# New instruction lists for the prologue and the first FFN half of a fused mixer and FFN kernel

## The reference

```python
uv = layernorm(x) @ in_proj_w + in_proj_b        # 512 -> 1024
u, v = uv[..., :512], uv[..., 512:]
v = silu(v); v_local = depthwise_conv3(v) + conv_b
h_t = a * h_(t-1) + ssm_b * v_local_t            # a = sigmoid(logit_a), along the rows
y = ssm_c * h + ssm_d * v_local
out = (u * silu(y)) @ out_proj_w + out_proj_b
attn = layernorm(out + layernorm(x)) * ln_w + ln_b
x = x + layernorm(attn)
z = gelu(layernorm(x) @ ternary(W1).T + b1)      # 512 -> 2048
x = x + layernorm(z @ ternary(W2).T + b2)        # 2048 -> 512
```

## Time and profile before

| what | value |
|---|---|
| time, median of 3 runs | 1447.07 us (1446.5 to 1452.28) |
| the profiled execution: its time | 1446.71 us |
| its span | 1444.7 us |
| busy PE, DVE, ACT, POOL | 97%, 77%, 61%, 30% |
| TensorE's mean granted clock | 0.995 of full speed |
| chain that ended last, by engine | PE 83%, DVE 6%, issue 4%, ACT 3% |

### The profile page before, as it was taken

The page is one execution under the profiler, slowest core; times in us unless marked ns, Lnnn a source line. Parts: engine busy times, 40 slices in busy tenths (PEclk is TensorE's granted clock), DMA queues, the critical chain, the costliest instruction groups (busy, mean ns, idle before and its releaser), DMA issues.

```text
span 1444.7 us, 18964 instructions
## 1 busy us (share of the span) xinstructions
PE 1402.6 (97%) x6492; PEld 637.3 (44%) x6492; DVE 1118.3 (77%) x1891; ACT 875.7 (61%) x1261; POOL 432.2 (30%) x522
## 2 busy tenths in 40 slices
...
GB/s 253 216 56 66 52 88 30 34 84 30 59 30 74 44 30 74 19 84 30 39 79 30 59 30 88 30 30 81 19 77 30 44 74 30 29 1 30 59 30 30
DMA packets 155984, 82.00 MB, mean 57 GB/s; under 512 B 132720, under 2 KB 132720, under 8 KB 155760
## 3 DMA queue, kind: packets, MB, share of 16 engines
...
## 4 chain that ended last, share of the span: by engine, by line
PE 83%; DVE 6%; issue 4%; ACT 3%; DMA 1%; POOL 1%; SPq 1%; DVEq 0%; POOLq 0%; ACTq 0%
PE f1b L534 14%; PE f1b L535 14%; PE f2b L562 13%; PE f2b L563 13%; PE misc L501 6%; PE misc L503 6%; PE misc L502 6%; PE misc L514 3%; PE misc L515 3%; PE misc L516 3%; DVE bn L696 1%; DVE tp L820 1%; POOL rsc L1624 1%; ACT ring L1293 1%; SPq L405 1%
## 5 line engine op out<-in xcount | busy, mean ns | idle before, releaser
L562 PE MATMUL f2b<-w,ring 128*128 128x512 fp8e5 x1008 | 382.7, 380 | 5.5 <-DVE w L1004 4.9
L563 PE MATMUL f2b<-w,ring 128*128 128x512 fp8e5 x1008 | 382.7, 380 | 0.0
L534 PE MATMUL f1b<-x3T,w 128*128 128x512 f16 x960 | 364.8, 380 | 4.0 <-DMA x3T<-tp 1.3
L535 PE MATMUL f1b<-x3T,w 128*128 128x512 f16 x960 | 364.8, 380 | 0.0
L1283 ACT ACTIVATE ring<-f1b,par 128x512 f32<-128x512 f32 x256 | 175.1, 684 | 249.7 <-PE f1b L535 249.4
L1623 POOL TENSOR_SCALAR ve<-mv 128x4 f32<-128x4 f32 (+2 forms) x89 | 33.7, 379 | 728.2 <-DVE mv L706 727.8
L714 DVE SCALAR_TENSOR_TENSOR ring<-ring,f_sc 128x512 f16<-128x512 f32 x256 | 208.8, 830 | 41.6 <-ACT ring L1293 41.6
L1293 ACT ACTIVATE ring<-ring,f_sc 128x512 f16<-128x512 f32 x256 | 180.4, 711 | 0.0
L501 PE MATMUL misc<-x1T,win_hi 128*128 128x512 f16 x464 | 175.9, 379 | 2.4 <-DVE yb L807 1.4
L502 PE MATMUL misc<-x1T,win_hi 128*128 128x512 f16 x464 | 175.9, 379 | 0.0
L503 PE MATMUL misc<-x1T,win_lo 128*128 128x512 f16 x464 | 175.9, 379 | 0.0
...
## 6 DMA issues: line engine op xcount, KB each, us to landing
...
x1T<-tp SPq DMA_TRANSPOSE x68, 3.1
...
```

The lines of the kernel that those rows point to most:

```text
L534: pe.matmul(b[:, :], w, src[:, k, :], start=k == 0, stop=False)
L535: mm = pe.matmul(b[:, :], w, src[:, KC + k, :], start=False, stop=k == KC - 1)
L562: pe.matmul(f2b[q][:, :], h_hi[:, i % H_SLOTS, qs], w2[:, j, :], start=j == 0, stop=False)
L563: mm = pe.matmul(f2b[q][:, :], h_lo[:, i % H_SLOTS, qs], w2[:, j, :], start=False, stop=j == FC - 1)
```

## The change

All five lists up to the second tile's u groups are written out instruction by instruction in a new order. On SP both u halves of `in_proj_w` are issued after all four transposes of tile 0, and the transposes of tile 1 ahead of `out_proj_w`, tile 2 and the first piece of W1; `load_w2(3)` goes behind the transposes of tile 2. On PE `warm` is called for 42 instead of 24 matmuls, the sum for the u half follows the second v group of tile 0, and the first FFN half has an order of its own (`first_ffn`). On DVE the chains are cut into named steps (`step` and `after` replace `link`), placed between other work; `wo_scale` no longer computes `o_inv`, which `wo_back` does later. Step 2's first half on DVE and ACT is listed instead of being sorted. Chunk 0 alone of W2 goes ahead of chunks 8 to 11 of W1. POOL computes the statistics of tile 0's blocks 2 and 3 together, and those of tile 2 after the edges. The core of the diff:

```diff
-ORDER = ([(W1_CHUNK, i) for i in range(8)] + [(W2_CHUNK, i) for i in range(4)] + [(W1_CHUNK, i) for i in range(8, 12)]
-         + [(W2_CHUNK, i) for i in range(4, 12)] + [(W1_CHUNK, i) for i in range(12, 16)]
-         + [(W2_CHUNK, i) for i in range(12, 16)])
-SIGNED = (1, 1, 1, 1, 2, 2, 2, 2, 3, 4, 5, 6, 7, 7, 7, 7, 8, 8, 8, 8, 9, 9, 9, 9, 10, 10, 10, 10, 11, 11, 11, 11)
-FIRST, SECOND = range(8, 21), range(28, 32)
-AT_TERNARY = {8: 1.19, 9: 2.25, 10: 3.3, 11: 3.5, 12: 5.11, 13: 5.12, 14: 5.7, 15: 5.75, 16: 6.3, 17: 6.4, 18: 6.6, 19: 7.4, 20: 7.6,
-              28: 11.55, 29: 11.6, 30: 11.65, 31: 14.55}
-AT_SIGN_C, AT_SIGN_Q, AT_SIGN_G, AT_SIGN_LAST = (0.5, 1.5, 2.5, 3.5), 4.4, (5.3, 6.5), 10.15
+ORDER = ([(W1_CHUNK, i) for i in range(0, 8)] + [(W2_CHUNK, i) for i in range(0, 1)]
+         + [(W1_CHUNK, i) for i in range(8, 12)] + [(W2_CHUNK, i) for i in range(1, 12)]
+         + [(W1_CHUNK, i) for i in range(12, 16)] + [(W2_CHUNK, i) for i in range(12, 16)])
+SIGNED = (1, 1, 1, 1, 2, 2, 2, 2, 3, 4, 4, 4, 4, 5, 6, 7, 8, 8, 8, 8, 9, 9, 9, 9, 10, 10, 10, 10, 11, 11, 11, 11)
+SECOND = range(28, 32)
+AT_TERNARY = {28: 11.55, 29: 11.6, 30: 11.65, 31: 14.55}
+AT_SIGN_LAST = 10.15
...
-for j in range(NB):
-    transpose("t1", 0, j)
-    if j < 2:
-        sp.dma_start(wf[:, 2 * j:2 * j + 2, 0:D], w_in_d[:, 2 * j:2 * j + 2, 0:D]).then_inc(winu_in[j], 16)
+transposes("t1", 0)
+for i in range(2):
+    sp.dma_start(wf[:, 2 * i:2 * i + 2, 0:D], w_in_d[:, 2 * i:2 * i + 2, 0:D]).then_inc(winu_in[i], 16)
+transposes("t1", 1)
 sp.dma_start(wo_raw, w_out_d).then_inc(wout_in, 16)
 load_x(2)
-transpose("t1", 1, 0)
 load_w1(0)
-for j in range(1, NB):
-    transpose("t1", 1, j)
 load_w1(1)
+sp.dma_start(row[:, :, :], rows.partition_broadcast(P)).then_inc(row_in, 16)
 load_w1(2)
-sp.dma_start(row[:, :, :], rows.partition_broadcast(P)).then_inc(row_in, 16)
 load_w1(3)
...
 load_w2(2)
-load_w2(3)
 transposes("t1", 2)
 load_w2(0)
 load_w2(1)
+load_w2(3)
 load_x(3)
...
     if (kind, t, b) == ("v", 1, 0):
         pe.wait_ge(par_ok, 4)
+    if (kind, t, b) == ("v", 1, 1):
         pe.wait_ge(scale_ok, 3)
...
-def setup_in_proj():
-    pe.wait_ge(x1_hi, 1)
-    warm(6)
-    pe.wait_ge(pmx, KC + 1)
-    pe.matmul(win_sum_bank(1), ones[:, :], wm_sq[:, 1, :], start=True, stop=True).then_inc(pm1, 1)
-    warm(6)
+def win_sum(half_):
+    pe.wait_ge(pmx, (KC + 4, KC + 1)[half_])
+    pe.matmul(win_sum_bank(half_), ones[:, :], wm_sq[:, half_, :], start=True, stop=True).then_inc(pm1, 1)
+def keep_warm():
     pe.wait_ge(x1_lo, 3)
-    warm(12)
-    pe.wait_ge(pmx, KC + 4)
-    pe.matmul(win_sum_bank(0), ones[:, :], wm_sq[:, 0, :], start=True, stop=True).then_inc(pm1, 1)
+    warm(14)
+    for k in (1, 3):
+        pe.wait_ge(win_l, k)
+        warm(8)
...
+def first_ffn():
+    f1(0, 0)
+    f1(0, 1)
+    f1(0, 2)
+    f1(0, 3)
+    f1(0, 4)
+    f1(0, 5)
+    f1(0, 6)
+    f2(0, 0)
+    f1(0, 7)
+    f1(0, 8)
+    f2(0, 1)
+    f2(0, 2)
+    f2(0, 3)
+    f2(0, 4)
+    f2(0, 5)
+    f2(0, 6)
+    f2(0, 7)
+    in_proj("u", 1, 2, u_mm)
+    in_proj("u", 1, 3, u_mm)
+    f2(0, 8)
...
 ffn_scale()
-setup_in_proj()
-for b in range(KC):
-    in_proj("v", 0, b, v_mm)
-for b in range(KC):
-    in_proj("v", 1, b, v_mm)
-    if b == 0:
-        wo_sum()
-for b in range(KC):
-    in_proj("u", 0, b, u_mm)
-for j in range(NB):
-    if j == NB - 1:
-        threshold(0)
-    o(0, j)
-for b in range(KC):
-    in_proj("v", 2, b, v_mm)
+pe.wait_ge(x1_hi, 1)
+warm(6)
+win_sum(1)
+warm(6)
+keep_warm()
+in_proj("v", 0, 0, v_mm)
+in_proj("v", 0, 1, v_mm)
+win_sum(0)
+in_proj("v", 0, 2, v_mm)
+in_proj("v", 0, 3, v_mm)
+in_proj("v", 1, 0, v_mm)
+in_proj("v", 1, 1, v_mm)
+in_proj("v", 1, 2, v_mm)
+wo_sum()
+in_proj("v", 1, 3, v_mm)
...
+o(0, 3)
+threshold(0)
...
+    steps[name] = len(steps) + 1
+def after(name):
+    ve_.wait_ge(prep, steps[name])
...
+        ve_.wait_ge(wo_sc_ok, 2)
...
 setup_params()
-for j in range(NB):
-    x_stats(0, j)
-    aggr(0, 0, j)
+x_stats(0, 0)
+aggr(0, 0, 0)
+x_stats(0, 1)
+x_stats(0, 2)
+aggr(0, 0, 1)
+x_stats(0, 3)
+aggr(0, 0, 2)
 win_max_v(0)
+aggr(0, 0, 3)
 win_max_v(1)
+win_max_v(2)
+win_max_v(3)
 t_lo("t1", 0, 0)
-win_max_v(2)
+win_square(1)
 t_lo("t1", 0, 1)
-win_max_v(3)
-win_square(1)
-t_lo("t1", 0, 2)
-win_scale(1)
-t_lo("t1", 0, 3)
+win_total(1)
 x_stats(1, 0)
-setup_split(0)
+win_power(1)
 x_stats(1, 1)
+win_bound(1)
 aggr(0, 1, 0)
 aggr(0, 1, 1)
-setup_split(1)
+win_scale(1)
+t_lo("t1", 0, 2)
 x_stats(1, 2)
-setup_split(2)
+t_lo("t1", 0, 3)
 x_stats(1, 3)
 aggr(0, 1, 2)
+setup_split(0)
 aggr(0, 1, 3)
+setup_split(1)
+setup_split(2)
+setup_split(3)
+t_lo("t1", 1, 0)
 v_scale()
-setup_split(3)
+t_lo("t1", 1, 1)
 win_max_u(0)
+t_lo("t1", 1, 2)
 win_max_u(1)
+t_lo("t1", 1, 3)
 win_square(0)
-t_lo("t1", 1, 0)
+taps(0, 0, True)
+win_total(0)
+win_power(0)
+win_bound(0)
 win_scale(0)
-t_lo("t1", 1, 1)
-t_lo("t1", 1, 2)
-setup_split(KC)
+ffn_total()
+taps(0, 1, True)
+setup_split(KC + 0)
+setup_split(KC + 1)
+ffn_exponent()
+ffn_inverse()
 ffn_scale()
-t_lo("t1", 1, 3)
+setup_split(KC + 2)
+taps(0, 2, True)
+gate_exponent()
 u_bias()
+gate_inverse()
+gate_shift()
+setup_split(KC + 3)
+gate_scale()
+gate_largest()
+taps(0, 3, True)
 x_stats(2, 0)
-setup_split(KC + 1)
-for j in range(1, NB):
-    x_stats(2, j)
-for j in range(NB):
-    aggr(0, 2, j)
-setup_split(KC + 2)
-gate_scale()
-taps(0, 0, True)
-taps(0, 1, True)
-setup_split(KC + 3)
-taps(0, 2, True)
-wo_scale()
+x_stats(2, 1)
...
+wo_norm()
+aggr(0, 2, 2)
+aggr(0, 2, 3)
 scan(0, 0)
 taps(0, 1, False)
+wo_total()
 y(0, 0)
-setup_out_proj(1)
+wo_power()
+taps(0, 2, False)
+wo_bound()
 scan(0, 1)
-taps(0, 2, False)
+wo_inverse()
+scan(0, 2)
 y(0, 1)
 taps(0, 3, False)
-setup_out_proj(2)
-scan(0, 2)
-ve_.wait_ge(par_ok, 8)
+wo_scale()
+ve_.wait_ge(par_ok, 5)
 gate(0, 0)
 y(0, 2)
-gate(0, 1)
+setup_out_proj(0)
...
+ternary(2)
+ternary(3)
+taps(1, 0, True)
+ternary(4)
+taps(1, 0, False)
+taps(1, 1, True)
+ternary(5)
+threshold_mean(1)
+scan(1, 0)
 threshold(1)
+y(1, 0)
 ternary(6)
 ternary(7)
+taps(1, 1, False)
+ternary(8)
+taps(1, 2, True)
+lo(0, 0)
+scan(1, 1)
+lo(0, 1)
+y(1, 1)
+taps(1, 2, False)
+ternary(9)
+ternary(10)
+ternary(11)
+ternary(12)
+ternary(13)
+ternary(14)
+scan(1, 2)
+lo(0, 2)
+y(1, 2)
+lo(0, 3)
+ternary(15)
+ternary(16)
+lo(0, 4)
+ternary(17)
+lo(0, 5)
+taps(1, 3, True)
+lo(0, 6)
+ternary(18)
+lo(0, 7)
+taps(1, 3, False)
+ternary(19)
+lo(0, 8)
+ternary(20)
+scan(1, 3)
+y(1, 3)
+gate(1, 0)
+gate(1, 1)
...
-        act.wait_ge(abs_ok, 6)
+        act.wait_ge(abs_ok, 8)
...
+t_hi("t1", 1, 3)
+silu_v(0, 0)
+centre_tap(0, 0)
+silu_v(0, 1)
+centre_tap(0, 1)
+split_in(KC + 0)
 split_in(KC + 1)
-silu_v(0, 0)
+silu_v(0, 2)
+split_in(KC + 2)
+centre_tap(0, 2)
+split_in(KC + 3)
+silu_v(0, 3)
+centre_tap(0, 3)
+silu_v(1, 0)
...
-t_hi("t1", 2, 2)
-front(2, 3)
+centre_tap(1, 0)
 abs_sum(4, 6, w2_raw[2], w2_in[2])
-centre_tap(1, 0)
-abs_sum(5, 7, w2_raw[3], w2_in[3])
+centre_tap(1, 1)
 sign_w1(0)
+abs_sum(5, 4, w2_raw[0], w2_in[0])
+abs_sum(6, 5, w2_raw[1], w2_in[1])
+silu_v(2, 0)
+abs_sum(7, 7, w2_raw[3], w2_in[3])
+silu_v(2, 1)
 sign_w1(1)
-centre_tap(1, 1)
-silu_v(2, 0)
-abs_sum(6, 4, w2_raw[0], w2_in[0])
-silu_v(2, 1)
 silu_v(2, 2)
-abs_sum(7, 5, w2_raw[1], w2_in[1])
-centre_tap(1, 2)
 silu_v(2, 3)
...
+copy_x3(7)
+load_table(1, ACT.Gelu)
+d_conv(1, 0)
+gelu(0, 0)
+centre_tap(1, 2)
+hi(0, 0)
+gelu(0, 1)
+sign_first(0)
+gelu(0, 2)
+hi(0, 1)
+hi(0, 2)
+gelu(0, 3)
+d_conv(1, 1)
+gelu(0, 4)
+sign_w1(2)
+gelu(0, 5)
+hi(0, 3)
+sign_first(1)
+sign_first(2)
+gelu(0, 6)
+d_conv(1, 2)
+sign_first(3)
+hi(0, 4)
+sign_w2(1)
+centre_tap(1, 3)
+gelu(0, 7)
+hi(0, 5)
+hi(0, 6)
+hi(0, 7)
+gelu(0, 8)
+hi(0, 8)
+sign_w2(2)
+d_conv(1, 3)
+silu_y(1, 0)
...
+rstd_first(0)
+rstd_first(1)
+rstd_x(0, slice(2, NB), front_rs)
 rstd_x(1, slice(0, 2), front_rs)
 rstd_x(1, slice(2, NB), front_rs)
 weight_bound()
 gate_bound()
+first_edge(0)
+first_edge(1)
+first_edge(2)
+first_edge(3)
+first_left()
 rstd_x(2)
-for b in range(KC):
-    first_edge(b)
-pool.tensor_copy(v[:, 1, :, 0:1], v[:, 0, :, TT:TT + 1]).then_inc(left_ok, 1)
-for b in range(KC):
-    keep_state(0, b)
-halves = slice(0, 2), slice(2, NB)
-for i, js in enumerate(halves):
-    rstd(1, 0, rsc[:, 0, js], True, js, (half_ok[1], rs_ok[1])[i])
-for i, js in enumerate(halves):
-    rstd_b_half(js, (half_ok[2], rs_ok[2])[i])
-for i, js in enumerate(halves):
-    rstd(3, 0, rsc[:, 2, js], True, js, (half_ok[3], rs_ok[3])[i])
+keep_state(0, 0)
+keep_state(0, 1)
+keep_state(0, 2)
+keep_state(0, 3)
+rstd_a_half(0)
+rstd_a_half(1)
+rstd_b_half(0)
+rstd_b_half(1)
+rstd_c_half(0)
```

More of the change, by code:

```diff
@@ L635, in _ @@
             pe.wait_ge(h_ok, NB)
-            for n in range(len(halves_x3)):
-                transpose_x3(n)
-                if n == 3:
-                    threshold(1)
+            transpose_x3(0)
+            transpose_x3(1)
+            transpose_x3(2)
+            transpose_x3(3)
+            transpose_x3(4)
+            threshold(1)
```

(31 more changed lines are left out.)

327 lines of the change are left out of this document (199 added, 128 removed).

## The result

The changed kernel takes **1439.62 us** (1438.39 to 1441.75, 12 runs) against 1446.49 for the kernel before beside it, 7 us less. The profiled execution took 1439.29 us with a span of 1436.6, which is 8.1 us less than the span before; by their times the two profiled executions differ by 7.4. The forecast was 1437.0 in a range of 1432 to 1444.

The account below looks back on a forecast made before the run. PE's own work bounds the kernel from 200 us on, so only earlier hand-over pays: 4.4 (front) + 7.1 (first FFN half) - 1.0 (clock) - 0.4 (hand-offs) = 10.1 us off 1446.7, said as 1437, range 1432 to 1444.

Parts of the forecast that it names:

- Start of PE: Tile 0's first v group on PE: starts at about 22.0, 0.9 us earlier, and 1.9 us more from full clock.
- u half behind the transposes: SP's later u loads: tile 0's transposes land earlier, so PE's 3.24 us hole at tile 1's v groups goes.
- Chains apart: DVE's scale chains split, 4.87 us hole filled: gate_lo of block 3 ends 4.4 us earlier, output projection starts at 57.1.
- The clock, mis-sized: PE idle 3.8 us before tile 0's output projection: clock falls, minus 1.0 us (bounds 0 and 1.9, perhaps twice).
- First FFN half: PE's stops for ternary chunks and slow matmuls behind them, 8.5 us, go; one new 1.4 us wait; net 7.1.
- Table load: Gelu table load on ACT between last copy and first gelu: takes 1.28 us, hidden, so costs nothing; otherwise 0.5 us.
- A: Rival: only the FFN half pays, the front's 4.4 us are lost to late loads or sums; 1441 us, chance 0.10.
- B: Rival: only the front pays, stops in the FFN half return at other places; 1443.7 us, chance 0.16.
- C: Rival: slower, the first FFN half runs in bursts at 1.2 GHz between holes; at most 1468 us, chance 0.06.

Follow-up runs that it names:

- less_warm: Changed kernel with 12 warm-up matmuls before the v groups instead of 14, 8 and 8; 1439.18 us.
- u_early: Changed kernel with SP's edit alone taken back: both u halves issued between the transposes of tile 0 again; 1438.41 us.
- u_sum_first: Changed kernel with the matmul for the u half's sum back ahead of the first v group on PE; 1443.19 us.
- old_half: Changed kernel with the first FFN half's old chunk order and old lists of PE, DVE and ACT; 1443.13 us.
- warm_x3: Changed kernel plus 12 dummy matmuls around the transposes of tile 0's FFN input on PE; 1437.22 us.
- warm_o: Changed kernel plus 11 dummy matmuls on PE before the first output projection; 1438.47 us.
- warm_both: Changed kernel with the dummy matmuls of both warm_o and warm_x3; 1435.89 us.
- new_half: Changed kernel with the old lists of all engines up to the first f1, keeping the new first FFN half; 1440.91 us.
- pe_order: Changed kernel with PE's first FFN half alone in the old interleaving, new chunk order and DVE and ACT lists kept; 1449.09 us.

## Why the prediction was right, and where it was not

The direction and the mechanism hold: what is handed over earlier before 200 us comes off the end. The size came out smaller, 8.1 of 10.1 us by span and 6.9 by the medians. Step by step:

*Start of PE.* Tile 0's v groups at 22.09 at full clock, said 22.0. The reason was wrong. I took the warm-up as what decides the start; it does, but `less_warm` starts at 19.34 with full clock and ends the same. An earlier start of the v groups pays nothing beyond what the later maxima allow. I also took the slow matmuls as worth 9 times 0.21, 1.9 us; by the row, nine of them took 3.60 us where full speed takes 1.94, which is 1.7.

*u half behind the transposes.* The hole of 3.24 us went, as said, and the wait for the u loads appeared (1.5 us). But on SP the move is worth nothing (`u_early`). What the new front cannot do without is the place of the u sum on PE (`u_sum_first`, 3.6 us), which I had listed under the start of PE.

*Chains apart.* The scan came 0.5 us earlier than walked (39.24, said 39.7), and `gate_lo` ended at 57.1, said 57.7. That filling the hole of 4.87 us is what brought this, no run shows by itself. The output projection started at 56.5, said 57.1. The thin cover of `threshold_sum(1)` held: it needed to be there at 79.2, and the sum started at 79.66 without a wait. The first f1 came at 90.28, said 89.4 with the 1.0 for the clock still to be added, so 90.4. That this is so near is partly luck: the output projection was 0.6 early, and the clock cost 1.4 instead of 1.0 (the 24 matmuls behind the hole of 2.90 us take from 56.51 to 63.38, 6.87 us instead of 5.2, and DVE waits 0.78 and 0.30 us at `h_add`). The 32.3 us that I had from the first `o` to the first f1 without it are what the traces with the clock held have. A wait of 0.61 us for POOL's `rsc`, which I had not listed, lies in the changed kernel, in `old_half` and in `warm_x3`.

*The clock, mis-sized.* This is the term that failed: "minus 1.0 (bounds 0 and 1.9, twice if the gap before f1 does the same)". I looked only at holes of over 3 us and found none before the first f1. The clock fell in the transposes, behind holes of 0.20 and 1.42 us between groups of small matmuls, with one of 0.78 still to come, and cost 2.0 us behind 90.28. In `old_half` and `warm_o` it was still at 1.00 behind the transposes and fell by the end of the last hole, of 0.98 and 1.19 us. The kernel before passed the same transposes at 1.00, with holes of 0.20, 0.74, 0.20 and 1.18 us. The term should have been 1.4 + 2.0 = 3.4; `warm_both` gives both parts back. By the Trainium skill, page TensorE: Matmul & The Clock Gate, on HAM oscillation, each burst of a kernel that waits between bursts starts slow; the trace agrees at this f1, behind waits much shorter than the ones I had applied it to, and does not agree for the same place before.

*First FFN half.* Said: 8.5 removed, one new wait of 1.4, net 7.1. Measured, with the clock's 2.0 out: 6.2; in `new_half` 5.7, and 6.0 in `warm_both` (49.4 us against 55.4). The three stops and the slow matmuls behind them, the 8.5, went. The new wait stood where I put it, before `u(1,2)`, with 0.76 us (1.28 in `new_half`). Two more of 1.12 and 0.76 at the second tile's output projection (132.05 and 136.88) were not in the walk; it ended at `gate(1,1)` and took DVE's operations behind it at their usual length. 8.5 - 0.76 - 1.12 - 0.76 is 5.9. So 1.9 us of waits are the second term that was too small, next to the clock. First `o` of that tile at 129.47, said 129.

*Table load.* It took 1.28 us, and the next ACTIVATE started 0.01 us behind it (91.44 after 90.15 and 1.28), so the price of the trace stood and not the 2.66 us of the Trainium skill, page ScalarE: Activation LUTs, What ACT_TABLE_LOAD costs.

*The rivals.* A (only the half pays) and B (only the front pays) are both refuted by `old_half` and `new_half`: each pays by itself. C, the slow half at 1.2 GHz, did not come in the changed kernel, but `pe_order` shows it in part: two stops of over 3 us, each followed by 1.2 GHz in the trace, and 10 us more, of which some 4 go with the clock. Its chance of 0.06 rested on PE's order, not on the lists alone.

The sum with the measured terms: 3.5 at the first f1 (with the first fall of the clock in it), 5.9 in the half by its stops and waits, minus 2.0 is 7.4; the trace has 7.7 at the last output projection of tile 1.
